# One scan rewritten inside a fused kernel: tanh and square written to PSUM, scales held in registers, a three-slot sum, and the linear terms redone on GpSimd

## The reference, cut to what matters

```
def _derivative(q, p, drive, coupling, bias):
    i_couple = jnp.tanh(q) @ coupling.T
    dq = q - q ** 3 / 3.0 - p + drive + i_couple + bias
    dp = EPSILON * (q + ALPHA - BETA * p)
...
# _rk4_step: four stages, each needs the q of the stage before
    dq1, dp1 = _derivative(q, p, drive, coupling, bias)
    dq2, dp2 = _derivative(q + 0.5 * DT * dq1, p + 0.5 * DT * dp1, drive, coupling, bias)
    dq3, dp3 = _derivative(q + 0.5 * DT * dq2, p + 0.5 * DT * dp2, drive, coupling, bias)
    dq4, dp4 = _derivative(q + DT * dq3, p + DT * dp3, drive, coupling, bias)
    q_next = clip(q + DT / 6.0 * (dq1 + 2 * dq2 + 2 * dq3 + dq4)); p_next = clip(...)
...
x = x + moe_ffn(scan(cond, cond, x))     # 8 experts, 2 chosen, and a shared one
```

## Time and profile before

| | us |
|---|---|
| median of 3 runs | 3337.66 (3329.26 to 3340.9) |
| the profiled execution, its own time | 3334.45 |
| its span, first to last instruction | 3332.7 |
| of it: layer 0, up to the first stage of the scan | 1029 |
| the 32 steps alone | 1029 to 1290 |
| seven groups of 32 steps with tiles | 1290 to 3172 |
| the last group of tiles, no scan | 3172 to 3333 |

### The profile page before, as it was taken

The page is one execution under the profiler, slowest core; times in us unless marked ns, Lnnn a source line. Parts: engine busy times, 40 slices in busy tenths (PEclk is TensorE's granted clock), DMA queues, the critical chain, the costliest instruction groups (busy, mean ns, idle before and its releaser), DMA issues.

```text
span 3332.7 us, 128510 instructions
## 1 busy us (share of the span) xinstructions
PE 3065.8 (92%) x46128; PEld 2574.2 (77%) x46128; DVE 1979.4 (59%) x6760; ACT 1166.1 (35%) x4210; POOL 1780.5 (53%) x3295
## 2 busy tenths in 40 slices
PE   6689999999994557999999999999999999999999
PEld 4257777787784446888888888888888888888887
DVE  2534543354325666777776777677677677677743
ACT  1122333233312334444444444344344344444410
POOL 0079996666644555555555555455455455555500
PEclk9589999999995556999999999999999999999999
DMA  4521111222210001333332323333333333333354
GB/s 160 147 73 54 54 54 47 85 76 79 81 61 20 0 0 36 101 98 102 96 102 97 102 94 101 97 101 97 100 98 94 102 98 102 95 103 94 101 170 160
DMA packets 118124, 294.17 MB, mean 88 GB/s; under 512 B 13904, under 2 KB 18512, under 8 KB 117584
## 3 DMA queue, kind: packets, MB, share of 16 engines
q1 hardware_dynamic: 117328, 288.83, 27.4%
q10 hardware_dynamic: 672, 3.67, 0.3%
HBM read 270.95 MB, written 21.50 MB: 88 GB/s over the span
## 4 chain that ended last, share of the span: by engine, by line
PE 39%; DVE 17%; issue 8%; ACT 4%; DVEq 1%; POOL 0%; DMA 0%; ACTq 0%; SPq 0%; POOLq 0%
PE pscan L927 11%; PE pg L855 10%; PE pscan L923 7%; PE pd L880 7%; DVE th L1059 4%; PE pu L855 4%; DVE state L1077 3%; ACT t L812 3%; DVE qraw L1077 2%; DVE pst L1072 2%; DVE trace L1085 2%; DVE cub L1061 2%; ACT th L811 1%; DVE pscan L1070 1%; DVE state L1080 0%
## 5 line engine op out<-in xcount | busy, mean ns | idle before, releaser
L923 PEld LDWEIGHTS pscan<-th,clo 128*128 128x128 f16 x16384 | 535.6, 97 | 245.6 <-ACT th L811 193.0
L923 PE MATMUL pscan<-th,clo 128*128 128x8 f16 x16384 | 565.4, 167 | 131.8 <-ACT th L811 131.6
L880 PE MATMUL pd<-hg,wd 128*128 128x256 f32 x2112 | 605.3, 394 | 1.1 <-DMA wd<-in_w_tiles 1.1
L927 PE MATMUL pscan<-th,chi 128*128 128x16 f16 x16384 | 571.5, 170 | 32.1 <-DVE th L1059 3.5
L811 ACT ACTIVATE th<-state,kp 128x32 f16<-128x32 f32 x768 | 246.9, 321 | 888.0 <-DVE state L1077 888.0
L1059 DVE TENSOR_TENSOR th<-t,th 128x32 f16<-128x32 f32 x1024 | 303.5, 296 | 386.6 <-ACT t L812 377.1
L927 PEld LDWEIGHTS pscan<-th,chi 128*128 128x128 f16 x16384 | 484.1, 97 | 60.0 <-DVE th L1059 52.3
L855 PE MATMUL pu<-qh,wgu 128*128 128x256 f16 x3168 | 464.9, 273 | 0.0
L855 PE MATMUL pg<-qh,wgu 128*128 128x256 f16 x3168 | 426.4, 274 | 13.1 <-issue 12.9
L880 PEld LDWEIGHTS pd<-hg,wd 128*128 128x128 f32 x2112 | 349.6, 193 | 27.3 <-issue 1.5
L855 PEld LDWEIGHTS pg<-qh,wgu 128*128 128x128 f16 x3168 | 294.2, 98 | 78.9 <-issue 14.9
(11 more groups left out here) (160 smaller groups left out, 4687.1 us busy)
## 6 DMA issues: line engine op xcount, KB each, us to landing
wgu<-w_split SPq DMA_DIRECT2D x264, 512.0 KB, 3.3
wd<-in_w_tiles SPq DMA_DIRECT2D x264, 256.0 KB, 2.7
half_in<-in_w_tiles SPq DMA_DIRECT2D x132, 256.0 KB, 2.7
w_split<-half_out SPq DMA_DIRECT2D x66, 256.0 KB, 2.0
hid<-in_up_q SPq DMA_DIRECT2D x8, 512.0 KB, 4.1
hid<-in_up_s SPq DMA_DIRECT2D x16, 256.0 KB, 5.2
hid<-in_dn_q SPq DMA_DIRECT2D x8, 512.0 KB, 3.7
hid<-in_dn_s SPq DMA_DIRECT2D x32, 128.0 KB, 3.8
```

Of the source, the lines that this page charges most:

```text
L880: ins = mm(pd[m // 2][:, (m % 2) * GT:(m % 2 + 1) * GT], wd[:, slot, m * P:(m + 1) * P], hg[:, slot, :], start=False, stop=False, skip_gro ...
L923: mm(pscan[:, 0, 0, m * B:(m + 1) * B], clo[:, k, m * P:(m + 1) * P], th[:, k, 0, :], start=(m == 0 and k == 0), stop=False, skip_group_ch ...
L927: ins = mm(pscan[:, 0, 0:2, m * B:(m + 1) * B], chi[:, k, m * P:(m + 1) * P], th[:, k], start=False, stop=(k == NC - 1), skip_group_check= ...
```

## The change

Everything is in `layer1`. `t32` moves from SBUF to a PSUM bank of its own (`pact`); `sq` and `cub` move to PSUM too, into the bank whose first slot takes the nonlinear and linear terms. ACT reads its scales once into registers. The sum takes three slots in one axis in place of four in two. Clipping p and clipping the state go from DVE to POOL; the copy into `trace` goes from DVE to ACT, is made from the clipped state at the start of the next step, and lands one slot later. POOL's linear terms are cut from 160 to 128 or 32 elements where a row is zero or can be folded into DVE's constant (`shift`). On DVE, `hidden_up` and `hidden_gate` go from `gap` to `late`, behind the sum of their stage.

```diff
-        t32 = sb("t32", [P, W])
-        sq = sb("sq1", [P, W]); cub = sb("cub", [P, W])
-        md, mp_ = (sb(n, [P, 5, W]) for n in ("from_drive", "from_p"))
+        md = sb("from_drive", [P, W])
...
-        pscan = ctx.enter_context(nc.psum_tensor("pscan", [P, 2, 512 // W, W], F32))
+        pscan = ctx.enter_context(nc.psum_tensor("pscan", [P, 4, 256], F32))
+        sq, cub = pscan[:, 3, 0:W], pscan[:, 3, W:2 * W]
+        pact = ctx.enter_context(nc.psum_tensor("pact", [P, 512], F32))
+        t32 = pact[:, 0:W]
...
 POOL, one step
+                pl.wait_ge(S["pchain"], at)
+                pl.tensor_tensor(A[u][:, 0:4, :], A[u][:, 0:4, :], rows(md[:], 4), ALU.add).then_inc(S["lin_ready"], 1)
                 pl.wait_ge(S["clip_ready"], t + 1)
                 pl.tensor_tensor(mq[:], rows(state[0][:], 4), cq[:, 1:5, :], ALU.mult).then_inc(S["pchain"], 1)
...
+                from_drive(t + 1)
                 pl.wait_ge(S["q_ready"], t * 4 + 3)
...
-                pl.tensor_tensor(ms4[:], rows(state[3][:], 2), c4[:], ALU.mult).then_inc(S["pchain"], 1)
-                pl.wait_ge(S["pchain"], at + 5)
-                pl.tensor_tensor(A[u][:, 3:5, :], A[u][:, 3:5, :], ms4[:], ALU.add).then_inc(S["e_ready"], 1)
+                pl.tensor_tensor(ms4[:], state[3][:], c4[:], ALU.mult).then_inc(S["pchain"], 1)
...
+                pl.tensor_tensor(ms4[:], ms4[:], A[u][:, 4, :], ALU.add).then_inc(S["pchain"], 1)
...
+                pl.tensor_scalar(pst[:], ms4[:], BETA * CLAMP - ALPHA, -BETA * CLAMP - ALPHA, ALU.min, ALU.max).then_inc(S["pchain"], 1)
+                pl.wait_ge(S["pchain"], at + 7)
+                from_p(1 - u)
+                pl.wait_ge(S["q_ready"], t * 4 + 5)
+                pl.sem_inc(S["plseq"], 1)
+                pl.tensor_scalar(state[0][:], qraw[:], kp[:, 8:9], kp[:, 9:10], ALU.min, ALU.max).then_inc(S["clip_ready"], 1)
 ACT
+            def held(name, ap):
+                reg = act.alloc_register(name)
+                act.reg_load(reg, ap.bitcast(I32))
+                return reg
+            units = [held(f"unit{s}", kp[0:1, 7:8] if s == 0 else kp[0:1, 3 + s:4 + s]) for s in range(4)]
...
-                        unit = kp[:, 7:8] if s == 0 else kp[:, 3 + s:4 + s]
+                        unit = units[s]
...
+                    if s == 0 and (scan or (first and u == 0)):
...
+                        act.activation(trace[:, :, bass.ds(slot, 1), :].rearrange("p c o b -> p c (o b)"), v3(state[0][:]), ACT.Identity).then_inc(S["traced"], 1)
 DVE
-                            gap.append(lambda: hidden_up(seg, n - 1, at == (1, 0)))
+                            late.append(lambda: hidden_up(seg, n - 1, at == (1, 0)))
                         if s == 1:
-                            gap.append(lambda: hidden_gate(seg, n - 1, 1 - u, gate_row(i, u)))
+                            late.append(lambda: hidden_gate(seg, n - 1, 1 - u, gate_row(i, u)))
...
-                        if s == 3:
-                            dve.tensor_scalar(pst[:], A[u][:, 4, :], BETA * CLAMP - ALPHA, -BETA * CLAMP - ALPHA, ALU.min, ALU.max).then_inc(S["pclip_ready"], 1)
...
-                        dve.tensor_reduce(nxt[:], pscan[:, :, 0:2, :].rearrange("p a s w -> p w a s"), AX.XY, ALU.add).then_inc(S["q_ready"], 1)
-                        if s == 3:
-                            dve.wait_ge(S["q_ready"], t * 4 + 5)
-                            dve.tensor_scalar(state[0][:], qraw[:], kp[:, 8:9], kp[:, 9:10], ALU.min, ALU.max).then_inc(S["clip_ready"], 1)
...
+                        dve.tensor_reduce(nxt[:], pscan[:, 0:3, 0:W].rearrange("p a w -> p w a"), AX.X, ALU.add).then_inc(S["q_ready"], 1)
```

More of the change, by code:

```diff
@@ L740, in _ @@
                 pl.memset(cq[:, r, :], float(coefs[r, 0] * RK[3] / unit))
-                for tile, col in ((cp, 1), (cd, 2)):
-                    pl.memset(tile[:, r, :], float(coefs[r, col] / unit))
+                pl.memset(cp[:, r, :], float(coefs[r, 1] / unit))
+                assert abs(coefs[r, 2] / unit - (r < 4)) < 1e-12
                 if r >= 2:
@@ L803, in _ @@
             act.wait_ge(S["scale_rdy"], 1)
+            def held(name, ap):
[3 more added lines that the diff above has]
+            units = [held(f"unit{s}", kp[0:1, 7:8] if s == 0 else kp[0:1, 3 + s:4 + s]) for s in range(4)]
+            half = held("half", wk[0:1, 3:4])
             def step(seg, i, u, t, scan, tile, old):
@@ L809, in step @@
                         act.wait_ge(S["q_ready"], t * 4 + s + 1)
-                        unit = kp[:, 7:8] if s == 0 else kp[:, 3 + s:4 + s]
+                        unit = units[s]
                         act.activation(th[:, :, 0, :], v3(src[:]), ACT.Tanh, scale=unit).then_inc(S["th_ready"], 1)
-                        act.activation(t32[:], src[:], ACT.Tanh, scale=unit).then_inc(S["t32_ready"], 1)
+                        act.activation(t32, src[:], ACT.Tanh, scale=unit).then_inc(S["t32_ready"], 1)
                         if s == 0:
                             act.wait_ge(S["clip_ready"], t + 1)
-                        act.activation(sq[:], state[s][:], ACT.Square, scale=unit).then_inc(S["sq_ready"], 1)
+                        act.activation(sq, state[s][:], ACT.Square, scale=unit).then_inc(S["sq_ready"], 1)
+                    first = tile and isinstance(i, int) and i == 0
+                    if s == 0 and (scan or (first and u == 0)):
+                        if not scan:
+                            act.wait_ge(S["clip_ready"], T + 1)
+                        if first and u == 1:
+                            act.wait_ge(S["q_low"], 2 * seg + 2)
+                        slot = G if first and u == 0 else 2 * i + u
+                        act.activation(trace[:, :, bass.ds(slot, 1), :].rearrange("p c o b -> p c (o b)"), v3(state[0][:]), ACT.Identity).then_inc(S["traced"], 1)
                     if tile:
@@ L838, in silu @@
                 act.wait_ge(S["gate_done"], n + 1)
-                act.activation(sg[:], pg[:, 0:GT], ACT.Tanh, scale=wk[:, 3:4]).then_inc(S["sg_ready"], 1)
+                act.activation(sg[:], pg[:, 0:GT], ACT.Tanh, scale=half).then_inc(S["sg_ready"], 1)
             walk(act, step, lambda seg: silu(seg * TILES + TILES - 1))
@@ L922, in step @@
                             for k in range(NC):
-                                mm(pscan[:, 0, 0, m * B:(m + 1) * B], clo[:, k, m * P:(m + 1) * P], th[:, k, 0, :], start=(m == 0 and k == 0), stop=False, skip_group_check=True)
+                                mm(pscan[:, 0, m * B:(m + 1) * B], clo[:, k, m * P:(m + 1) * P], th[:, k, 0, :], start=(m == 0 and k == 0), stop=False, skip_group_check=True)
                         pe.wait_ge(S["tl_ready"], t * 4 + s + 1)
```

75 lines of the change are left out of this document (35 added, 40 removed).

## The result

The changed kernel takes 3211.01 us (median of 4 runs, 3209.8 to 3220.34), the kernel before 3335.43 us on the same chip (4 runs, 3329.26 to 3340.9): a ratio of 0.9639, with a 95% interval of 0.9617 to 0.966 (the two medians by themselves give 0.9627). Predicted were 3217. The profiled execution is the longest of the four (3220.34). Layer 0, whose code did not change, ended 5.9 us later in it than in the profiled execution of before, so the two profiles differ by 114.2 us of span where the medians differ by 124.

What follows compares the result with a forecast made beforehand. PE's own work nearly bounds regular tile steps, a stage's chain the steps alone. 3334.45 - 76 - 34 - 10 + 1 = 3215 us, predicted as 3217 because the profiled execution lies 3 under the median; 8-in-10 range 3178 to 3275.

Steps and rivals of the forecast that it cites:

- Regular tile steps: 210 steps in 7 groups: all of PE's waits, 0.36 us a step, go; 8.04 to 7.67 us, 76 us saved.
- My split of PE's work: Tile steps, chi of stage 0 to chi of stage 2: 3.78 us of PE work, estimated as 1.97 and 1.81.
- The cause of the wait in stage 0: Tile steps: DVE's low part, held by a POOL instruction, takes 0.48 us; chi comes 0.66 after clo, an excess of 0.26.
- Steps alone: The first 32 steps: a step falls from 8.05 to 6.98 us, saving 34 us; bounds 25 and 44.
- The stage of 1.71: One stage alone, from one sum's start to the next: 1.71 us, with PE reaching chi after the low part is ready.
- The 0.28 in every second step for POOL's loop turn: Steps alone: at POOL's loop turn the first sum is held from 1.45 to 1.73 us, 0.14 on the mean.
- First two steps of a group: Group starts, bound by PE and the router's chain on DVE by turns: 1.5 us saved a group, 10 us in all.
- PE gets to what it waited for a little earlier: First two steps of a group: a reason given for their gain, bounds 0 and 4 us a group.
- Setup: Before the first step: five register loads on ACT cost 1 us.
- wait moved in behind the sum: Rival, chance 0.14: hb, hg or POOL delays the low part, PE waits 0.3 us in each tile step: 3293 us.
- became the bound: Rival, chance 0.04: POOL's linear rows come too late for DVE in stage 0 of tile steps; ends slower.
- The clock: Rival "more is won", chance 0.15: PE's half clock comes up alone, or stages bound group starts more; 20 to 40 us more, 3185.

Runs made afterwards that it cites:

- p1_less_up: The changed kernel with two of the 12 up products in each tile left out on PE (output not the reference's): 3160.0 us, a tile step 7.42.
- b3_drive: The kernel before with only POOL's drive product of the next step moved from behind the terms of stage 3 to behind those of stage 1: 3356.2 us.
- e1_pointers: The changed kernel with the scales of tanh and square as pointers to SBUF again: 3223.1 us, ratio 0.966 to the kernel before.
- c1_both: The kernel before with two parts of the change, operands t32, sq and cub in PSUM and scales in registers: 3225.8 us, ratio 0.9671.
- w1_warm: The changed kernel with three matmuls added behind each chi in the 32 steps alone, result unchanged: 3214.5 us, ratio 0.9635 to the kernel before.
- e2_sbuf: The changed kernel with t32, sq and cub in SBUF again: 3225.3 us, ratio 0.9667 to the kernel before.

## Why the prediction was right, and where it was wrong

The total was right, by 6 us in 3217, and part of that is luck: two terms were 7 and 5 us too small and one 12 too large, and these misses cancel. The mechanism of the two large terms is borne out. The terms, in the profiled execution:

- **Regular tile steps**, -76 predicted: 210 x 0.396 = -83. "All of PE's waits go" holds, and p1_less_up shows that PE alone bounds the step. The wait was 0.40 and not 0.36. My split of PE's work, 1.97 and 1.81, is 1.97 and 1.78 in the trace.
- **The cause of the wait in stage 0** was half read. "The cause in stage 0 stands on DVE" named the held low part and took POOL's late `lin` as given. It was late because the clip of p was itself held for 0.61 by a product that began 0.03 us earlier, which no row of mine showed; with that clip free and all else as before (b3_drive), chi of stage 0 starts 0.40 behind clo. The order of parts that I implied, PSUM for the tile steps and registers for the steps alone, is wrong: from the kernel before, each takes away most of the same wait (89 and 77 of 109 us). The total came out right because it rested on PE's floor and not on the sum of the parts.
- **Steps alone**, -34 predicted: 32 x 1.22 = -39. The stage of 1.71 was exact, register, sum and PE's pace each at their price (ACT 321 to 229 ns as e1_pointers shows, the sum 0.258). The 0.28 in every second step for POOL's loop turn didn't come. POOL's linear add starts as the clip of the state ends, in each step that I read, so the turn fits into the time in which POOL waits for the sum or runs the clip; that is read from the trace, and no run tests it.
- **First two steps of a group**, -10 predicted: +2, counted from clip to clip over all seven groups (each of the last five loses between 0 and 1.2 us, the first, which follows the steps alone, gains 1.7). Here a step of mine failed: "PE gets to what it waited for a little earlier" was to win time. PE does get there earlier: at the boundary at 2117 us of before it reaches chi 0.65 and 1.12 us after clo in two stages, and at the one at 2049 us of the changed kernel 0.40 to 0.41 in every stage but the two at half clock. But PE's clock takes that back. Granted clock in the 27 us ahead of the cleared down product, at two boundaries of before, then of the changed kernel:

```profile
2090.40:2117.40 27.00, 25.12 (x398) 21.77 (x399) 19.43 (x78) 10.91 (x38) 9.56 (x23) 0.87 0.29 91
...
2902.60:2929.60 27.00, 25.06 (x398) 21.72 (x399) 19.43 (x78) 10.93 (x38) 9.84 (x23) 0.87 0.28 91
```

```profile
2021.70:2048.70 27.00, 26.08 (x398) 22.70 (x400) 17.21 (x73) 8.54 (x41) 9.34 (x26) 0.81 0.27 90
...
2800.10:2827.10 27.00, 26.10 (x399) 22.77 (x401) 16.78 (x73) 8.54 (x41) 9.37 (x26) 0.81 0.28 90
```

  A mean of 0.87 costs 0.13 x 27 = 3.5 us of full clock, one of 0.81 costs 5.1. Five of the six boundaries of before stand at 0.87, five of six at 0.81 after. So 1.6 us of clock at each, less the 0.5 that a group's first two steps lose (29.4 against 28.9), leave a gain of about 1.1 that the clock eats up; this 1.1 is a difference, and no row shows it. The kernel c1_both has both kinds in one execution: its groups that end in a boundary at 0.87 take 258.3 and 258.2 us, those at 0.82 and 0.83 take 260.0, 260.2 and 259.9. So has w1_warm, whose groups run the changed kernel's code: 258.0 and 258.1 at 0.87, 259.7, 259.5 and 259.1 at 0.81. That the time goes with the clock, and by about as much as the clock accounts for, is shown by this; what decides between the two kinds is open, since no run changed only that.
- **Setup**, +1: +1.8, from 0.25 to 2.0 us between DVE's last setup instruction and the first tanh. The 5.9 us of layer 0 are no part of the change.

The rivals: no wait moved in behind the sum; e2_sbuf shows what it looks like (0.09 in every second step) where the operands are not in PSUM. POOL never became the bound. The clock did not come up by itself in the steps alone; it does with six more matmuls behind each chi, and then gives 6 to 8 us and not 20 to 40. One small price was wrong without harm: a small clip on POOL takes 0.36 and not 0.29.

## What to carry to other kernels

Where DVE and POOL both work from SBUF on small tiles, look at the start times, not only at mean durations: an instruction that comes 0.03 us behind POOL's pays all of POOL's time, and any change of a few hundredths, an unrelated one too, can free it or move the hold elsewhere. Putting one operand in PSUM ended it for these three instructions. Moving the POOL instruction, or making it smaller, made another hold in the two runs that tried it (21 us lost, 54 won). When several parts of a change attack waits of one engine, add up what that engine must do, and take it as the floor: parts that give 89 and 77 alone gave 109 together.
